# A graph attention layer on one core: p in two float32r words instead of three bfloat16 words, and TensorE adds the gathered q of three heads instead of two

## The reference

```
feats = relu(x @ W1 + b1) @ W2 + b2                      # per head: 256 -> 256 -> 64
hid   = relu(concat(feats[row], feats[col], elem) @ A1 + ab1)   # 129 wide
e     = leaky_relu(hid @ A2 + ab2, 0.2);  w = exp(e - max(e))
pooled = segment_sum(w * feats[col], row);  row_sum = segment_sum(w, row) + 1e-10
h      = pooled / row_sum                                # row = src, col = dst
out = layernorm(x + concat of the four heads' h)
```

## Time and profile before

| | |
|---|---|
| median of 3 runs | 4876.15 us (4874.23 to 4877.1) |
| the profiled execution: its span, from the first to the last instruction | 4828.3 us |
| busy: TensorE, VectorE, ScalarE, GpSimd | 4260.4, 4460.2, 3835.5, 2693.5 us |
| mean granted TensorE clock | 0.977 of full speed |
| moved by DMA | 851.82 MB, mean 176 GB/s |

### The profile page before, as it was taken

The page is one execution under the profiler, slowest core; times in us unless marked ns, Lnnn a source line. Parts: engine busy times, 40 slices in busy tenths (PEclk is TensorE's granted clock), DMA queues, the critical chain, the costliest instruction groups (busy, mean ns, idle before and its releaser), DMA issues.

```text
span 4828.3 us, 133194 instructions
## 1 busy us (share of the span) xinstructions
PE 4260.4 (88%) x24114; PEld 3004.1 (62%) x24115; DVE 4460.2 (92%) x25378; ACT 3835.5 (79%) x12983; POOL 2693.5 (56%) x2886
## 2 busy tenths in 40 slices
PE   1598998898896999999999999999999999999990
PEld 1355555555555777777777777777777777777760
DVE  8799999999996999999999999999999999999998
ACT  1587778778774888888888888888888888888884
POOL 5366666666664555555555555555555555555544
PEclk9999999999997999999999999999999999999995
DMA  2133333333334877777777777777777777777757
GB/s 85 43 73 86 79 71 80 81 77 80 79 76 137 240 225 221 228 225 224 224 225 224 225 225 221 226 224 224 225 224 224 224 225 225 225 225 225 221 172 212
DMA packets 266918, 851.82 MB, mean 176 GB/s; under 512 B 107916, under 2 KB 109584, under 8 KB 266861
## 3 DMA queue, kind: packets, MB, share of 16 engines
q0 software_dynamic: 169920, 673.54, 50.0%
q1 hardware_dynamic: 63543, 160.18, 11.2%
q10 hardware_dynamic: 33398, 17.49, 1.4%
HBM read 739.10 MB, written 111.90 MB: 176 GB/s over the span
## 4 chain that ended last, share of the span: by engine, by line
PE 36%; ACT 27%; issue 3%; DVE 2%; DMA 1%; ACTq 0%; POOL 0%; DVEq 0%; SPq 0%; POOLq 0%
ACT z L1164 18%; PE psum L971 15%; PE psum L975 9%; PE psum L958 8%; ACT onehot L1193 3%; ACT onehot_t L1182 3%; PE psum L984 3%; ACT onehot L1197 2%; PE psum L939 1%; DVE z L1689 1%; DVE z L1682 0%; PE psum L995 0%; ACT onehot L1195 0%; DVE z L1705 0%; DMA p_win<-p_table 0%
## 5 line engine op out<-in xcount | busy, mean ns | idle before, releaser
L754 POOL DMA_INDIRECT z<-qf_table,rec x1664 | 1609.2, 967 | 1454.9 <-PE psum L958 1027.1
L1164 ACT ACTIVATE z<-z 128x64 f32<-128x64 f32 x6656 | 1651.1, 335 | 0.0
L971 PE MATMUL psum<-p_win,onehot_t 128*128 x9984 | 1407.8, 274 | 84.1 <-ACT onehot_t L1182 68.3
L971 PEld LDWEIGHTS psum<-p_win,onehot_t 128*128 128x128 bf16 x9984 | 966.8, 97 | 540.0 <-issue 214.4
L958 PE MATMUL psum<-z,onehot 128*128 128x260 f32 x3328 | 1029.4, 391 | 6.7 <-DVE acc L1617 4.9
L975 PE MATMUL psum<-z,ident 128*128 128x258 f32 x3328 | 1002.7, 383 | 0.0
L1568 DVE SCALAR_TENSOR_TENSOR z<-z,a_b 128x129 f32<-128x129 f32 x3328 | 884.3, 290 | 5.6 <-issue 0.2
L1568 DVE SCALAR_TENSOR_TENSOR z<-psum,a_b 128x129 f32<-128x129 f32 x3328 | 828.2, 286 | 0.0
L1558 DVE TENSOR_TENSOR z<-z,psum 128x258 f32<-128x258 f32 x1664 | 698.6, 420 | 94.6 <-PE psum L975 90.6
L1617 DVE TENSOR_TENSOR acc<-acc,psum 125x260 f32 x1664 | 702.3, 422 | 25.3 <-PE psum L958 2.4
L695 POOL DMA_INDIRECT sorted_rows<-z x300 | 478.5, 1595 | 403.9 <-DVE z L1447 321.6
(11 more groups left out here) (220 smaller groups left out, 5576.3 us busy)
## 6 DMA issues: line engine op xcount, KB each, us to landing
p_table<-acc SPq DMA_DIRECT2D x100, 338.6 KB
p_win<-p_table SPq DMA_DIRECT2D x100, 338.6 KB
z<-qf_table,rec POOLq DMA_INDIRECT x1664, 4.5
qf_table<-acc SPq DMA_DIRECT2D x75, 339.5 KB
acc<-in_x_dram SPq DMA_DIRECT2D x25, 448.0 KB
z<-in_x_dram SPq DMA_DIRECT2D x20, 560.0 KB
out_dram<-z ACTq DMA_DIRECT2D x20, 560.0 KB
qf_table<-z SPq DMA_DIRECT2D x25, 339.5 KB
```

What stands on the lines that cost most here:

```text
L754: pool.indirect_dma_start(out=z_t[:, o + j, :], out_offset=None, in_=qf_table, in_offset=bass.IndirectOffsetOnAxis(ap=rec[:, o + j, 3:4].b ...
L971: mm = pe.matmul(to, onehot_t[:, j, :], p_flat[:, bass.ds((w % 2) * (3 * ZW) + (part * ZW + o), n)], start=(part == 0), stop=(part == 2 an ...
L1164: op = act.activation(z_t[:, slot, o:o + DO], z_t[:, slot, o:o + DO], ACT.Copy, scale=z_t[:, slot, o + DO:o + HF])
```

## The change

p is kept as two words in float32r: the high word is p rounded to that format, the low word the float32 rest. `p_table`, `p_win`, `onehot_t` and the copies of A1's last row change format; a row of p is 4128 bytes. TensorE makes two products for each half of 258 columns instead of three, and adds q for three heads (387 columns) instead of two; VectorE adds it for one (129 columns), and takes three dots from PSUM and one from `z`. GpSimd's four operations a window become one subtraction (`low_part`); ScalarE makes the high word (`high_part`). Some small tables move within SBUF, and the window tables are copied by a DMA before the edge stage starts.

```diff
-    PEH = 2
-    NA = (H - PEH) * AT if PEH else HALF
-    NB = ZW - NA
+    PEH = 3
+    NA = (H - PEH) * AT
...
-        p_win = sb("p_win", [P, 2, 3 * ZW], BF16)
+        p_win = sb("p_win", [P, 2, 2 * ZW], F32R)
...
-        onehot_t = sb("onehot_t", [P, SB, P], BF16)
+        onehot_t = sb("onehot_t", [P, SB, P], F32R)
...
             sp.wait_ge(s_tab_step, N_TAB_STEPS)
+            sp.wait_ge(s_acc_zero, 1 + BULK)
+            sp.dma_start(tables, tables_made).then_inc(s_tab_st, 16)
             sp.wait_ge(s_rec_st, 16 * BULK)
...
-            def split_p(g, w):
+            def low_part(g, w):
 
                 n, b = g * 4 + w, w % 2
-                pf = p_f[0:WN, b, :]
-                pool.wait_ge(s_p_ev, n + 1)
-                since(pool, s_p_st[b], g * 64 + w // 2 * 32)
+                pool.wait_ge(s_p_hi, n + 1)
                 pool.sem_inc(s_passed, 1)
-                pool.tensor_copy(p_out[0:WN, b, 0:ZW], pf).then_inc(s_p_hi, 1)
-                pool.wait_ge(s_p_hi, n + 1)
-                pool.tensor_tensor(pf, pf, p_out[0:WN, b, 0:ZW], ALU.subtract).then_inc(s_p_rest, 1)
-                pool.wait_ge(s_p_rest, n + 1)
-                pool.sem_inc(s_passed, 1)
-                pool.tensor_copy(p_out[0:WN, b, ZW:2 * ZW], pf).then_inc(s_p_mid, 1)
-                pool.wait_ge(s_p_mid, n + 1)
-                pool.tensor_tensor(p_out[0:WN, b, 2 * ZW:3 * ZW], pf, p_out[0:WN, b, ZW:2 * ZW], ALU.subtract).then_inc(s_p_lo, 1)
-
-            order = [(split_p, -1, 3), (scatter, 0, 0), (scatter, 0, 1), (scatter, 0, 2), (split_p, 0, 0), (split_p, 0, 1),
-                     (scatter, 0, 3), (split_p, 0, 2)]
+                pool.tensor_tensor(p_out[0:WN, b, ZW:2 * ZW], p_f[0:WN, b, :], p_out[0:WN, b, 0:ZW], ALU.subtract).then_inc(s_p_lo, 1)
+
+            order = [(low_part, -1, 2), (low_part, -1, 3), (scatter, 0, 0), (scatter, 0, 1), (scatter, 0, 2), (low_part, 0, 0),
+                     (scatter, 0, 3), (low_part, 0, 1)]
...
-                    for o, n, to in ((0, NA, z_one(slot)), (NA, NB, z_two(slot))):
-                        for part in range(3):
-                            mm = pe.matmul(to, onehot_t[:, j, :], p_flat[:, bass.ds((w % 2) * (3 * ZW) + (part * ZW + o), n)],
-                                           start=(part == 0), stop=(part == 2 and not (o and PEH)), skip_group_check=True)
-                    if PEH:
-                        pe.wait_ge(s_gather[slot], i * 16 + 16)
-                        mm = pe.matmul(z_two(slot), ident[:, :], z_t[:, slot, NA:ZW], start=False, stop=True, skip_group_check=True)
-                    mm.then_inc(s_z_mm, 1)
+                    for u in range(2):
+                        for part in range(2):
+                            pe.matmul(z_half(slot, u), onehot_t[:, j, :], p_flat[:, bass.ds((w % 2) * (2 * ZW) + (part * ZW + u * HALF), HALF)],
+                                      start=(part == 0), stop=False, skip_group_check=True)
+                    pe.wait_ge(s_gather[slot], i * 16 + 16)
+                    pe.matmul(z_half(slot, 0)[:, NA:HALF], ident[:, :], z_t[:, slot, NA:HALF], start=False, stop=True, skip_group_check=True)
+                    pe.matmul(z_half(slot, 1), ident[:, :], z_t[:, slot, HALF:ZW], start=False, stop=True, skip_group_check=True)\
+                      .then_inc(s_z_mm, 1)
...
+            def high_part(g, w):
+
+                n, b = g * 4 + w, w % 2
+                act.wait_ge(s_p_ev, n + 1)
+                since(act, s_p_st[b], g * 64 + w // 2 * 32)
+                act.activation(p_out[0:WN, b, 0:ZW].bitcast(F32R), p_f[0:WN, b, :], ACT.Copy).then_inc(s_p_hi, 1)
...
-                    if PEH:
-                        own = z_t[:, slot, 0:NA]
-                        dve.tensor_tensor(own, own, z_one(slot), ALU.add).then_inc(s_z_added, 1)
-                        for h in range(H - PEH, H):
-                            op = dot(slot, h, z_two(slot)[:, h * AT - NA:(h + 1) * AT - NA])
-                        op.then_inc(s_z_free, 1)
...
+                    own = z_t[:, slot, 0:NA]
+                    dve.tensor_tensor(own, own, z_half(slot, 0)[:, 0:NA], ALU.add).then_inc(s_z_added, 1)
+                    for h in range(H - PEH, H):
+                        op = dot(slot, h, z_head(slot, h))
+                    op.then_inc(s_z_free, 1)
```

More of the change, by code:

```diff
@@ L27 @@
 BF16 = mybir.dt.bfloat16
+F32R = mybir.dt.float32r
 AX_X = mybir.AxisListType.X
@@ L81, in gnn_layer @@
     qf_table = nc.dram_tensor("qf_table", (N, QW), F32, kind="Internal").ap()
-    p_table = nc.dram_tensor("p_table", (N, 3 * ZW), BF16, kind="Internal").ap()
+    p_table = nc.dram_tensor("p_table", (N, 2 * ZW), F32, kind="Internal").ap()
     CHUNKS = NT * P // S
@@ L215, in gnn_layer @@
         iota_s = carve_z(S // 2).bitcast(BF16)
+        iota_win = carve_z(W // 2).bitcast(BF16)
         ident_b = carve_z(P // 2).bitcast(BF16)
+        ones_b = carve_z(P // 2).bitcast(BF16)
+        before = carve_z(P // 2).bitcast(BF16)
         before_f = carve_z(P)
@@ L1105, in take_q @@
                                psum[0:WN, 2:4, HALF:HALF + P].rearrange("p q (r f) -> p q r f", r=2), ACT.Copy).then_inc(s_q_ev, 1)
-            beside = {0: [(take_x,)], 1: [(take_h, 0)], 2: [(take_h, 1)], 3: [(take_h, 2)], 4: [(take_h, 3)], 5: [(take_h, 4)], 6: [(take_h, 5)],
-                      7: [(take_f, 0), (take_h, 6)], 8: [(take_h, 7)], 9: [(take_f, 1)], 10: [(take_q, 0)], 11: [(take_q, 1)],
-                      12: [(take_q, 2)], 13: [(take_q, 3)]}
+            def high_part(g, w):
[3 more added lines that the diff above has]
+                act.activation(p_out[0:WN, b, 0:ZW].bitcast(F32R), p_f[0:WN, b, :], ACT.Copy).then_inc(s_p_hi, 1)
+            beside = {0: [(0, take_x)], 1: [(-1, high_part, 2), (0, take_h, 0)], 2: [(0, take_h, 1)], 3: [(-1, high_part, 3), (0, take_h, 2)],
+                      4: [(0, take_h, 3)], 5: [(0, take_h, 4)], 6: [(0, take_h, 5)], 7: [(0, take_f, 0), (0, take_h, 6)], 8: [(0, take_h, 7)],
+                      9: [(0, take_f, 1)], 10: [(0, take_q, 0)], 11: [(0, take_q, 1)], 12: [(0, take_q, 2)], 13: [(0, take_q, 3), (0, high_part, 0)],
+                      15: [(0, high_part, 1)]}
             def group(g):
@@ L1121, in group @@
                         take_rows(g, b)
-                    for work, *args in beside.get(q, []):
-                        if not isinstance(g, int) or g < GROUPS:
-                            work(g, *args)
+                    for off, work, *args in beside.get(q, []):
+                        if not isinstance(g, int) or 0 <= g + off < GROUPS:
+                            work(g + off, *args)
             act.dma_start(base_rows_d[:, :, :].rearrange("h u n -> h (u n)"), base_hl[0:BLOCKS, :].bitcast(BF16)).then_inc(s_base_st, 16)
@@ L1573, in own_dot @@
                     if h == 0:
-                        dve.wait_ge(s_z_added if PEH else s_z_free, tile(0, j) + 1)
+                        dve.wait_ge(s_z_added, tile(0, j) + 1)
                     op = dot(slot, h, z_t[:, slot, h * AT:(h + 1) * AT])
```

81 lines of the change are left out of this document (36 added, 45 removed).

## The result

The changed kernel takes 4954.95 us (median of 4 runs, 4952.05 to 4955.93), the kernel before beside it 4875.31 us: a ratio of 1.016, 95% interval 1.0146 to 1.0175. It is slower by 80 us, where I had forecast 95 us faster (4781 against 4876.15).

The account below looks back on a forecast made before the run. The edge stage was taken as bound by a ScalarE-TensorE loop (change 0), the sort by TensorE and VectorE in turn (95 us saved): 4828.3 - 95 = 4733, plus 47.9 gives 4781 us; own range 4735 to 4815, 8 in 10 4700 to 4910.

Parts of the forecast that it names:

- The premise: Sort and node stage: VectorE's excess of 182 us comes from GpSimd's arithmetic on p holding it up.
- three quarters: Sort: of a group's four windows, three are split while VectorE sets the pace, so 127 x 3/4 = 95 us saved.
- 0.48 us for each; 115.4 us leave 55.: Sort: 182 us excess over 381.9 us of GpSimd arithmetic; one subtraction of 115.4 us leaves 55, so 127 go.
- my lower case: Sort: every subtraction left blocks VectorE for its whole time; 67 us of stall go, 50 on the path.
- New waits: Sort: ScalarE waits for p_sum and the store, p_sum for the low part; about 1 us room each, else up to 25 us.
- Rival (d): Sort: VectorE's relief is worth nothing, filled by ScalarE's or the store's new waits, or TensorE: 4866 to 4880 us; 8%.
- The loop ScalarE to TensorE to ScalarE: Edge stage: this loop, with three hidden_src and two evictions, sets the period of 15.07 us; VectorE is in no link.
- terms of 0.22 and 0.44 us: Edge stage: TensorE's float32 products of 129 and 258 columns in one hidden_src, 0.66 us together.
- The float32r product: Edge stage: 0.11 us each on TensorE, four per hidden_src; 1.10 us against 1.10, so 0 change.
- rival (b): Edge stage: weight loads not quite hidden, 0.13 to 0.16 us a product: 4825 to 4905 us; 10%.
- Rival (a): Edge stage: a float32r product costs a float32 pass, 0.22 us: about 5180 us; 11%.
- 47.9 us above the span, and moves with it: Whole run: the median 4876.15 us lies 47.9 above the profiled span 4828.3; added to 4733, it gives 4781.

Follow-up runs that it names:

- before_small_split: The kernel before with GpSimd's four operations a window on 2 columns instead of 516, work left out: 4751.48 us, ratio 0.9746.
- high_on_gpsimd: The changed kernel with the high word made by GpSimd ahead of its subtraction, not by ScalarE: 4869.08 us, level with the kernel before (1.0002).
- again_before: The kernel before, unchanged, profiled a second time: 4868.95 us, span 4867.2.
- low_before_scatter: The changed kernel with window 1's low_part ahead of the scatter of block 3 in GpSimd's order: 4885.68 us.

## Why the prediction was wrong

**The sort, forecast -95, measured +50.7 us.** The premise stood (before_small_split), and so did the size of the share, three quarters. Two steps failed.

*"0.48 us for each; 115.4 us leave 55."* I spread VectorE's excess evenly over GpSimd's time. Measured, the excess went from 184 to 142, not to 55. The rows of the changed kernel, 150 to 1600 us:

```profile
L1438 DVE TENSOR_SCALAR acc<-z 125x320 bf16<-125x320 bf16 x1600 | 516.2, 385 | 0.3 <-issue 0.3
L710 POOL TENSOR_TENSOR acc<-acc 125x516 f32<-125x516 f32 x100 | 141.5, 1556 | 191.0 <-ACT acc L1109 122.0 <-issue 69.0
```

The comparisons' mean hardly fell (388 to 385 ns, where I had looked for 330). The subtractions take 141.5 us, not 115.4 (the shortest is 1.27 us against 1.09 of L708), and VectorE lost as much: 1.0 us for each. In high_on_gpsimd it is 0.68, before 0.48. The trace of before shows what the even rate hid. There a comparison beside one of these operations is held until the operation ends:

```profile
840.03 1.09 POOL L708 TENSOR_TENSOR acc<-acc 125x516 f32<-125x516 f32 x1
840.24 0.99 DVE L1433 TENSOR_SCALAR acc<-z 125x320 bf16<-125x320 bf16 x1
```

A cast of 0.62 us there holds a comparison for 0.65 in the same way. The average was low because a held comparison would have taken 0.3 us anyway, and because the operations often lay beside other work: summed over the records of again_before, L708 has a comparison beside it for 111 of its 116 us, the casts L706 and L711 for 53 of 93 and 31 of 62, and L713 for 28 of 113. What counts is thus what runs beside an operation, not its share of GpSimd's time: in low_before_scatter the same 100 subtractions at other places cost 0.87 us for each. Two subtractions cost the most where the second starts before the first has ended: the changed kernel has 25 such pairs, the records of each overlap by some 0.57 us, and each holds one comparison through both. In again_before 231 operations follow the one ahead within 0.1 us, with an overlap of 0.06 at most, and none of these holds a comparison through two; the longest is 1.21 us. What lets a pair overlap no run tells.

The result was my lower case, "if every subtraction left blocked VectorE for its whole time", at its bound. The Trainium skill, "SBUF — State Buffer", section SBUF: two separate sides, has one of the two engines hold the shared ports for a whole instruction while the other blocks. That would have been the better guide; the 0.99 us beside 1.09 agree with it. At three quarters, 42 us less excess are worth -31 us. (The range's upper end has a slip too: a gain of 50 ends at 4826 us, not at 4815.)

*"New waits: by estimate each has about 1 us of room. If it is gone: up to 1 us a group, 25 us."* This is the larger failure: -31 forecast by the measured excess, +50.7 found, 82 us, 3.3 us for each of 25 groups. I had seen that window 1's low word, which "stands behind three indirect DMAs", is late, and had priced it only as a wait of `p_sum`. What it does is to overlap with window 2's, and so to hold one comparison for 3.6 us, after which TensorE runs out of work. The clock is low for what follows, for longer than before. Moving it gives 69 us, moving ScalarE's wait nothing that shows. My place for the wait was right, its cause was not: it is late because VectorE is. Rival (d) named ScalarE's waits too, but had them at most use up the gain. A part stays open: the sort of low_before_scatter is 19.7 us quicker than before's, where three quarters of its 59 us less excess would be 44.

**The edge stage, forecast 0, measured +36.0 us.** The loop ScalarE to TensorE to ScalarE stood in the changed kernel; its terms of 0.22 and 0.44 us stood. The float32r product was taken at 0.11 us and is 0.12: the mechanism of rival (b), just below its range of 0.13 to 0.16. (15.24 - 15.08) x 207 = 33 us; the other 3 lie in the long periods below. The sizes were nearly right, but 0.01 us was multiplied by 12 products and 207 super-blocks, which is 25 of the 33 us; the other 8 are what a product of 0.123 us would add. Rival (a), a product of 0.22 us, is out. Eviction, windows and the tables' DMA cost nothing that shows.

**VectorE's idle time** was no reserve worth buying: the 0.23 us a tile that the third head costs TensorE lay on the loop, what it saves VectorE did not. As two changes the words (with the sort that comes with them) are worth -23 us, or -106 with the high word on GpSimd, the third head costs 107 to 154 us.

**The base.** "47.9 us above the span, and moves with it" was no property of the kernel but of one quick execution. It did not enter the difference.

## What to carry to other kernels

Removing work from an engine that blocks another is not enough: what counts is what the rest of it runs beside. Look in the trace for two such operations whose records overlap: in a row but not overlapping they held a comparison for 1.23 us at most in the kernel before, overlapping for 3.66. And ask what the blocked engine's consumer does meanwhile, since a TensorE gap of 4 us was followed by 6 us at a mean clock of 0.72. And if a change joins several edits, price each against the loop alone; here the words alone, with the high word on GpSimd, gave 2.2%, and the whole change cost 1.6%.

## What I had not expected of the hardware

Both kernels pause on GpSimd between two gathers every 170 us or so, in the changed kernel 16 times from 2000 to 4600 us:

```profile
2697.25 0.95 POOL L751 DMA_INDIRECT z<-qf_table,rec  x1 [3.31 <-PE psum L955]
```

In the quick execution of before this was absorbed: there all periods but one stay at 15.13 us or below, and the first two were 13.1 and 12.2. In its second profile some super-blocks beside such pauses take 15.7 to 16.5 us, and the first two 27.5 and 20.7; the changed kernel's mostly take 16 to 17.1, and its first two 26.7 and 19.2. That is where the 36.9 us between the edge stages of two executions of one kernel lie. No run here tells what sets the pauses off, nor why one execution escapes their cost.
